# The four running sums of the second attention in eight scans instead of four

## The reference

```python
q, k, v = jnp.split(qkv, 3, axis=-1)
q = rms_norm(q)
k = rms_norm(k)
w = jnp.exp(k)
kv = w * v
w = jnp.cumsum(w, axis=1)
kv = jnp.cumsum(kv, axis=1)
y = kv / (w + 1e-06)
y = jax.nn.sigmoid(q) * y
```

## Time and profile before

| what | value |
|---|---|
| median of three runs | 5370.36 us (5359.03 to 5375.56) |
| the profiled execution | 5370.94 us |
| its span, first to last instruction | 5369.1 us |
| TensorE busy (matmul) | 4723.8 us, 88% |
| VectorE busy | 3857.4 us, 72% |
| ScalarE busy | 3387.7 us, 63% |
| GpSimd busy | 4016.2 us, 75% |
| mean granted TensorE clock | 0.888 of full speed |
| the 16 scans of line 1728 | 31.3 us busy, mean 1964 ns |
| the 16 scans of line 1733 | 37.4 us busy, mean 2349 ns |

### The profile page before, as it was taken

The page is one execution under the profiler, slowest core; times in us unless marked ns, Lnnn a source line. Parts: engine busy times, 40 slices in busy tenths (PEclk is TensorE's granted clock), DMA queues, the critical chain, the costliest instruction groups (busy, mean ns, idle before and its releaser), DMA issues. The chain is left out here.

```text
span 5369.1 us, 69474 instructions
## 1 busy us (share of the span) xinstructions
PE 4723.8 (88%) x21278; PEld 1826.6 (34%) x21278; DVE 3857.4 (72%) x4448; ACT 3387.7 (63%) x4022; POOL 4016.2 (75%) x2368
## 2 busy tenths in 40 slices
PE   8669999998999899988989998999899978569998
PEld 4311112223223222322222222222322334458886
DVE  6868888888988898889888988988898830500112
ACT  6655667778777877787777777777877643111112
POOL 0079999998999899989988998999899900343332
PEclk9855559988999899899989998999899989589999
DMA  3367677776777677767776776777677712245555
GB/s 128 124 229 251 243 248 241 272 257 238 251 267 260 231 260 256 267 224 250 269 247 235 258 266 245 251 255 266 234 255 260 250 51 63 79 168 177 177 177 184
DMA packets 316663, 1189.59 MB, mean 222 GB/s; under 512 B 77296, under 2 KB 114928, under 8 KB 305296
## 3 DMA queue, kind: packets, MB, share of 16 engines
q1 hardware_dynamic: 292736, 1067.95, 58.0%
q0 software_dynamic: 23568, 117.21, 6.3%
HBM read 1129.61 MB, written 89.19 MB: 227 GB/s over the span
## 5 line engine op out<-in xcount | busy, mean ns | idle before, releaser
L1616 POOL TENSOR_TENSOR s_h<-s_decay,s_h 128x768 f32<-128x768 f32 x2048 | 3710.6, 1856 | 296.2 <-ACT s_decay L1274 285.8
L1657 DVE TENSOR_TENSOR s_h<-s_h,bank 128x1024 f32<-128x1024 f32 x2048 | 2468.6, 1215 | 402.4 <-POOL s_h L1616 215.3
L1274 ACT ACTIVATE s_decay<-s_decay,s_a_neg 128x1536 f32<-128x1536 f32 x1024 | 1606.4, 1569 | 219.7 <-DMA s_decay<-dt_rows 218.8
L907 PE MATMUL bank<-s_h,s_cdiag 128*32 128x512 f32 x8192 | 1256.8, 689 | 9.9 <-ACT s_y L1286 9.2
L1279 ACT ACTIVATE bank<-bank,s_a_neg 128x512 f32<-128x512 f32 x1024 | 671.9, 656 | 638.9 <-PE bank L895 635.9
L881 PE MATMUL bank<-s_vrow,s_brow 9*128 9x512 bf16 x4096 | 844.2, 423 | 261.8 <-DVE s_h L1657 223.0
L881 PEld LDWEIGHTS bank<-s_vrow,s_brow 9*128 9x128 bf16 x4096 | 208.8, 92 | 1483.3 <-issue 1479.9
L1647 DVE TENSOR_TENSOR s_h<-bank,s_h 128x512 f32<-128x512 f32 x1024 | 698.1, 682 | 9.5 <-issue 8.2
L1019 PE MATMUL bank<-m_mb,m_w 128*128 128x512 f32 x1024 | 521.4, 638 | 0.9 <-ACT m_mb L1352 0.9
L1005 PE MATMUL bank<-m_ma,m_w 128*128 128x512 f32 x1024 | 516.4, 633 | 0.0
L895 PE MATMUL bank<-s_drow,s_unit 3*128 3x512 bf16 x1024 | 433.3, 424 | 56.1 <-DMA s_drow<-dt_parts 48.2
(11 more groups left out here) (232 smaller groups left out, 4095.9 us busy)
## 6 DMA issues: line engine op xcount, KB each, us to landing
s_decay<-dt_rows SPq DMA_DIRECT2D x1024, 768.0 KB, 5.6
m_w<-in_units SPq DMA_DIRECT2D x208, 512.0 KB, 5.4
s_vrow<-v_parts SPq DMA_DIRECT2D x1024, 36.0 KB
slots<-in_fill SPq DMA_DIRECT2D x512, 64.5 KB, 4.5
s_brow<-b_parts SPq DMA_DIRECT2D x1024, 9.0 KB
v_parts<-p_part SPq DMA_DIRECT2D x24, 512.0 KB, 3.0
m_w<-w_scaled SPq DMA_DIRECT2D x16, 512.0 KB, 5.1
e_got<-expert_out SPq DMA_DIRECT2D x8, 1024.0 KB, 7.1
```

What stands on the lines that cost most here:

```text
L907: mm = pe.matmul(bank[q * 32:(q + 1) * 32, Y0], cdiag[:, hf * LANES + q, at * BLK:(at + 1) * BLK], h[:, t % 2, hf * LANES + q], start=(at ...
L1274: act.activation(decay[:, k % RING], decay[:, k % RING], ACT.Exp, scale=a_neg[:, 1:2]).then_inc(decay_ok, 1)
L1616: pool.tensor_tensor(h[:, t % 2, g * PAIR:(g + 1) * PAIR, DCOLS:], decay[:, k % RING, g % 2 * PAIR:(g % 2 + 1) * PAIR], h[:, (t + 1) % 2, ...
L1657: dve.tensor_tensor(h[:, t % 2, g * PAIR:(g + 1) * PAIR], h[:, t % 2, g * PAIR:(g + 1) * PAIR], bank[:, X0 + n % 2 * PAIR:X0 + (n % 2 + 1) ...
```

## The change

Each scan of 520 elements is made as two of 260, four sequences each. `halves` cuts the tiles, `hf` says which half, and only the second half gives the signal that ScalarE and `divide` wait for. The two halves stand two slots apart: slot 80 becomes 79 and 81, 87 becomes 86 and 88, 99 becomes 98 and 100, 108 becomes 106 and 108. In `keys_tail` the halves stand back to back. No other engine's program is touched.

```diff
--- before.py
+++ after.py
@@ -551,8 +551,8 @@
 ROOT_Y_AT = 4
 ROOT_QK_AT = 12
 Y_GATE_AT = (13, 15, 17, 21)
-CW_AT = (80, 87)
-CKV_AT = (99, 108)
+CW_AT = (79, 81, 86, 88)
+CKV_AT = (98, 100, 106, 108)
 SEED_AT = 19
 KEEP_AT = (54, 68)
 DEN_AT = (114, 124)
@@ -1720,18 +1720,25 @@
                 dve.tensor_tensor(by_batch(u_runs[:, 4 + c]), by_batch(u_runs[:, c]),
                                   tiles_by_batch(bank[:, 4 + c if tail else M0]), ALU.mult).then_inc(S("kv_ok"), 1)
 
-            def sum_weights(m, c):
+            halves = (lambda a, hf: a[:, hf * RUNS // 2:(hf + 1) * RUNS // 2])
+
+            def sum_weights(m, c, hf):
                 dve.wait_ge(S("seeded"), FIRST + m * 2 + 1)
                 dve.wait_ge(S("ew_ok"), FIRST + m * KD + c + 1)
                 dve.wait_ge(S("qk_n"), FIRST + (m + 1) * 2 * TT)
                 dve.wait_ge(S("qT_ps"), FIRST + (m + 1) * KD)
-                dve.tensor_tensor_scan(cw(c), mask[:], u_runs[:, c], 0.0, ALU.mult, ALU.add).then_inc(S("cw_ok"), 1)
-
-            def sum_values(m, c):
+                part = dve.tensor_tensor_scan(halves(cw(c), hf), halves(mask[:], hf), halves(u_runs[:, c], hf), 0.0,
+                                              ALU.mult, ALU.add)
+                if hf == 1:
+                    part.then_inc(S("cw_ok"), 1)
+
+            def sum_values(m, c, hf):
                 dve.wait_ge(S("seeded"), FIRST + m * 2 + 2)
                 dve.wait_ge(S("kv_ok"), FIRST + m * KD + c + 1)
-                dve.tensor_tensor_scan(ckv(c), mask[:], u_runs[:, 4 + c], 0.0, ALU.mult, ALU.add
-                                       ).then_inc(S("ckv_ok"), 1)
+                part = dve.tensor_tensor_scan(halves(ckv(c), hf), halves(mask[:], hf), halves(u_runs[:, 4 + c], hf), 0.0,
+                                              ALU.mult, ALU.add)
+                if hf == 1:
+                    part.then_inc(S("ckv_ok"), 1)
 
             def denominator(m, c):
                 dve.wait_ge(S("kept"), FIRST + m * 2 + 1)
@@ -1788,9 +1795,9 @@
                 if n - 1 in UP_AT:
                     hidden(m, UP_AT.index(n - 1), False)
                 if attn and n in CW_AT:
-                    sum_weights(m - 1, CW_AT.index(n))
+                    sum_weights(m - 1, *divmod(CW_AT.index(n), 2))
                 if attn and n in CKV_AT:
-                    sum_values(m - 1, CKV_AT.index(n))
+                    sum_values(m - 1, *divmod(CKV_AT.index(n), 2))
                 if attn and n in DEN_AT:
                     denominator(m - 1, DEN_AT.index(n))
                 if attn and n in REC_AT:
@@ -1838,9 +1845,11 @@
                 for c in range(KD):
                     weigh(m, c, True)
                 for c in range(KD):
-                    sum_weights(m, c)
+                    for hf in range(2):
+                        sum_weights(m, c, hf)
                 for c in range(KD):
-                    sum_values(m, c)
+                    for hf in range(2):
+                        sum_values(m, c, hf)
                 for c in range(KD):
                     denominator(m, c)
                 for c in range(KD):
```

## The result

The changed kernel takes 5361.72 us (median of 16 runs, 5337.54 to 5372.59), the kernel before 5370.60 (16 runs, 5359.03 to 5382.43). The ratio is 0.9976, with a 95% interval of 0.9965 to 0.9987: **faster by 0.24%**. That is 13 us by the ratio and 9 us by the medians. Two repeats of the changed kernel, on two chips, gave 0.9982 [0.9968, 0.9996] and 0.9988 [0.9971, 1.0005]; the second by itself can't be told from no change. Over all runs of this study, 33 of the changed kernel and 123 of the one before, the medians are 5360.7 and 5370.4 us, 9.6 us apart.

A forecast was written before the change was run, and what follows sets the result against it. GpSimd's decay product was the tightest repeated operation, in a rhythm of 1.78 us per slot. Terms 0.6 - 2.4 + 9.6 - 5.2 + 1.4 + 0.6 = +4.6 us on 5370.94 gave 5375 us, range 5357 to 5390.

The forecast's parts named there:

- GpSimd stretched: GpSimd products beside scans: eight half scans at 0.49 us, 3.9 us per chunk against 3.8 before; +0.6 us for six chunks.
- The hole: GpSimd's idle stretch before slot 88: the half scan at slot 86 runs there and stretches no product; -2.4 us.
- The second wait: VectorE further behind at slots 91, 100 and 108, delaying ScalarE's activation and the exponential GpSimd waits for; +9.6 us.
- The clock: TensorE's clock falls after the scan of slot 108: two thirds go with the stall cut in two; -5.2 us.
- Long waits: Two-input VectorE instructions passed over by GpSimd products: 24 more requests at 2/170 and 5 us each; +1.4 us.
- The tail: Back-to-back scans in the tail: each pays one more start, about half hidden by overlap; 8 scans, +0.6 us.
- each half waits like a whole: Slower rival: lag at slots 91, 100, 108 exceeds ScalarE's spare time and new stalls bring clock falls; +19, 5390 us, chance 0.17.
- Clock stays up and the lag is swallowed: Faster rival: shorter stalls, both kinds of TensorE clock fall go, the second wait costs nothing; -9.8, 5361 us, chance 0.17.
- Passed over more often: Slower rival: the new scan requests bring one to three more long waits behind GpSimd; 5379 to 5389 us, chance 0.08.
- Nothing but a cut: Same-time rival: all waits shrink with the scan, slot order does not matter; only stretch and tail terms, 5372 us, chance 0.08.

## Why the prediction was wrong

The mechanism stood as told: a scan begins when the product in flight ends, and the product behind it is stretched. Point by point:

1. **GpSimd stretched** (+0.6, bounds -3.6 to +6). A half stretches by 0.40 us, not 0.49. The denominator of 512 elements was not the right neighbour: it works as long as a half scan alone (0.67 us), but stretches a product by 0.46. Why the same work stretches less in a scan, no run here shows. A whole scan stretches by 0.93, a half by 0.40, a quarter by 0.13, where they work 1.18, 0.67 and 0.41 alone. Eight at 0.40 against four at 0.93 is -0.5 us per chunk, -3 us: the lower bound, nearly.
2. **The hole** (-2.4). Right: 0.68 us at slot 86, nothing stretched, 0.40 x 6 = 2.4.
3. **The second wait** (+9.6). The times on VectorE came as foreseen, 2.35 us at slots 88, 98 and 106 and 1.19 at 100 and 108. What GpSimd saw of them in a chunk without a fall at 88 was about 0.2 at slot 88 and 0.1 to 0.15 at 98, not 0.8 and 0.3: some 0.3 us per chunk, +2. The share that I let TensorE and ScalarE swallow was far too small. One thing behind it was missed: in 6 of 18 chunks the stall at slot 88 takes the clock down and drags further falls behind it, at 15.3 - 10.9 = 4.4 us each, two per execution, +9 us. By chance that is the size of the term. It is also what the change would gain in these slots if every chunk were a quiet one: 12.4 - 10.9 = 1.5 us per chunk, 9 us per execution.
4. **The clock** (-5.2, falls after 108 two thirds gone). They went from 15 of 18 to 8, a half, and those after slot 87 or 88 from 12 to 6. In the first chunk the waits before 118 and 124 are 0 and 0.64 instead of 0.36 and 1.84, as the price of 1.56 us had it. With that price the falls that went are 6 x 7/18 x 1.56 + 6 x 6/18 x 0.44, about -4.5 us, the size of the term. But that they are worth it is not shown: the two chunks of the change whose only fall is behind slot 108 wait 1.18 us before slot 124, and in slots 76 to 151 they take 10.4 and 10.7 us, no more than the chunk without any fall (10.8). Those two falls last 3.4 us, 14 of the 15 of before 6.8 us or more, so it may be the longer ones that cost. The new falls behind slot 131, in 9 of 18 chunks, stand behind a reciprocal that I never looked at. They cost nothing that the chunks show.
5. **Long waits** (+1.4, bounds 0 to +5). **This step failed**, in sign and size. I put all two-input instructions into one rate, 2 in 170, and held that more requests mean more long waits. In the traces whole scans are passed over 12 times in 96, and halves and quarters never in 432. Three per execution at 3.6 us are 10.8 us in the traces of before, and none are left in those of after. In the two traces of before that are near the median it is 1.5 per execution, about 5 us. The bound had no room for a gain, though the same rows showed one such wait in 24 scans already in use, which the change could take away. The Trainium skill's rule (SBUF — State Buffer, Who interferes with whom), by which whichever issued first blocks the other, would make this term zero: the runs speak against that, as the 7.01 us did.
6. **The tail** (+0.6). The four halves of one line take 2.46 and 2.44 us there, where two whole scans took 2.36: +0.2 per tail, about +0.4.

Without the long waits the forecast's terms said +3.2 us. The sizes found are -3 - 2.4 + 2 + 9 - 4.5 + 0.4 = +1.5, and the slots themselves show 12.4 - 12.4 = 0 per chunk, with the tail about 0. So the sum was off by some 3 us in everything except the term of 1.4 us, which was -11 in these traces. Together that is -11, against -9.6 by the medians of all runs. The agreement is closer than the traces can vouch for: with 1.5 long waits per execution the same sum is -5.

Of the rivals, *each half waits like a whole* (5390) describes the back-to-back cut, which took 5399. *Clock stays up and the lag is swallowed* (5361) has the right time, but by luck: the falls did not all go, and in that sum the long waits were still +1.4. *Passed over more often* is refuted: a cut scan was not passed over once. *Nothing but a cut* (5372), by which the order of slots doesn't matter, is refuted by the back-to-back run.

Shown by the runs: both parts of the change are needed, the scans' contention costs some 22 us, halves and quarters are not passed over where whole scans are, and in the six traces the gain in slots 76 to 151 is that of the passed-over scans. Argued only: how much of the 9.6 us they are in a usual execution, since the mean of three rests on one execution, of 5406.91 us, with six. Open: **why** a scan is passed over. Length matters at slot 98 (3 of 6 whole scans, 0 of 24 halves, asked for at the same moment), but it alone is not the rule, since a swiglu product near slot 180 that works 0.69 us alone, as long as a half scan, was passed over in 10 of 84 cases (5.86 us, has one).

## What to carry to other kernels

A VectorE instruction that has to wait for GpSimd's products pays once for its length and once for being asked for. In this kernel halves gained only where they stood two slots apart, and in a hole of GpSimd (slot 86) a half cost no wait; back to back they cost 27 us, and quarters gave the gain back. A single odd duration in one trace, such as 7.01 us in 24, is a rate: profile a second and third time before it is priced, look where each profiled execution lies among the runs (5406.91 us, with six of them, was the slowest of eight), and ask of such a cost first whether the change takes it away. And when a stall that took TensorE's clock down is removed, look for the next stall behind it, since the wait may only move (1.88 us from slot 124 to 142, and from there to 150).

## What the runs showed of the hardware

- A waiting two-input VectorE instruction is not always served when GpSimd's product ends. It can be passed over until GpSimd runs dry: 6.4 to 7.0 us for whole scans in 12 of 96 cases, 5.85 to 5.88 us for a product of 512 elements in 10 of 84, never for scans of 260 or 130 elements (0 of 432).
- The product behind is stretched by less than the scan's own time: 0.93 of 1.18 us, 0.40 of 0.67, 0.13 of 0.41.
- A multiplication of one float32 tile by a number per partition contends (1.42 and 2.04 us on average), a maximum over one tile does not (0.687 us every time).
- An idle time of TensorE does not by itself say whether its clock falls. In the changed kernel TensorE idled 2.06 to 2.23 us behind slot 88 in 18 of 18 chunks; in six of them 3.4 to 6.8 us at 1.2 GHz followed, in twelve none. The longest such stretch in slots 76 to 151 was 10.2 us (among others in the second trace of before, behind a scan passed over at slot 108, and with the halves back to back).
